# Four stacked graph layers on one core: a score lookup with the table as the stationary operand, edge scores moved into an earlier stage, and another split of the gathered groups

## What is computed

```
xp = (x @ W).reshape(n, 3, 128)
a_src = einsum('nhc,hc->nh', xp, att_src);  a_dst likewise
a_edge = einsum('ehc,hc->eh', (edge_attr @ W_edge), att_edge)     # edge_attr has 16 columns
alpha = a_src[row] + a_dst[col] + a_edge;  alpha = leaky_relu(alpha, 0.2)
m = segment_max(alpha, col);  ex = exp(alpha - m[col]);  attn = ex / segment_sum(ex, col)[col]
agg = segment_sum(attn * xp[row], col)
out = layer_norm(x + agg.reshape(n, 384) @ lin_W + lin_b)
```

## Time and profile before

| | us |
|---|---|
| median of three runs | 3340.34 |
| lowest and highest run | 3336.01, 3341.25 |
| profiled execution, first to last instruction | 3527.6 |
| PE busy in it | 2502.7 (71%) |
| DVE busy | 1567.2 (44%) |
| POOL busy | 1419.9 (40%) |
| ACT busy | 704.3 (20%) |

### The profile page before, as it was taken

How to read it: one execution, slowest core, us unless ns; L and a number is a source line. 1 busy time by engine, 2 the same in 40 slices (tenths; PEclk the granted TensorE clock), 3 DMA queues, 4 the chain that set the end, 5 groups by cost and what they waited for, 6 DMA issues and landing times. The chain is left out here.

```text
span 3527.6 us, 68807 instructions
## 1 busy us (share of the span) xinstructions
PE 2502.7 (71%) x21724; PEld 2132.1 (60%) x21725; DVE 1567.2 (44%) x3759; ACT 704.3 (20%) x1093; POOL 1419.9 (40%) x1498
## 2 busy tenths in 40 slices
PE   1599999898899828999699815555555105888865
PEld 0466666686788617888588714444444105888854
DVE  5476766333111461111333345555545662444467
ACT  0187878353100321000100000000000010000033
POOL 4322222123000031222244466666665786666655
PEclk9899999998999959999899956666666555555577
DMA  4388888722988348888699846555555344555511
GB/s 123 95 251 284 283 275 283 251 73 57 288 284 281 107 124 266 250 246 248 194 287 296 236 139 142 132 137 136 134 134 138 96 128 115 128 128 129 131 41 43
DMA packets 560770, 627.34 MB, mean 178 GB/s; under 512 B 265887, under 2 KB 412524, under 8 KB 560041
## 3 DMA queue, kind: packets, MB, share of 16 engines
q1 hardware_dynamic: 258425, 387.60, 35.8%
q10 hardware_dynamic: 252072, 164.25, 17.0%
q0 software_dynamic: 50208, 74.70, 9.1%
HBM read 484.61 MB, written 142.11 MB: 178 GB/s over the span
## 5 line engine op out<-in xcount | busy, mean ns | idle before, releaser
L893 POOL DMA_INDIRECT rows<-x_rows,src_i x832 | 842.9, 1013 | 477.0 <-issue 224.3
L1567 PE MATMUL ps<-slices,wide 128*128 128x250 f16 x7350 | 829.2, 271 | 57.6 <-DVE wide L2246 34.1
L1567 PEld LDWEIGHTS ps<-slices,wide 128*128 128x128 f16 x7350 | 716.4, 98 | 146.1 <-DVE wide L2246 50.4
L1792 PE MATMUL ps<-slices 128*128 128x75 bf16 x4992 | 343.3, 242 | 340.3 <-issue 324.4
L1792 PEld LDWEIGHTS ps<-slices 128*128 128x128 bf16 x4992 | 294.2, 127 | 389.4 <-issue 388.4
L933 POOL TENSOR_TENSOR ea_one<-ea,ones 128x64 f32<-128x64 f32 x250 | 134.0, 537 | 459.9 <-DMA ea<-in_edge_attr 450.3
L1507 PE MATMUL ps<-weighted,slices 128*128 128x57 f32 x1120 | 254.4, 418 | 82.0 <-issue 72.6
L1507 PEld LDWEIGHTS ps<-weighted,slices 128*128 128x128 f32 x1120 | 247.4, 332 | 83.4 <-issue 73.9
L1453 PE MATMUL ps<-rows,weighted 128*32 128x128 f32 x2000 | 273.3, 281 | 14.8 <-DMA ea<-in_edge_attr 12.9
L1453 PEld LDWEIGHTS ps<-rows,weighted 128*32 128x32 f32 x2000 | 203.1, 112 | 60.3 <-issue 51.9
L2546 DVE TENSOR_TENSOR hT<-ps,hT 128x600 f32<-128x600 f32 x104 | 81.1, 780 | 324.5 <-remote 229.3
(11 more groups left out here) (356 smaller groups left out, 3463.4 us busy)
## 6 DMA issues: line engine op xcount, KB each, us to landing
slices<-adjacency SPq DMA_DIRECT2D x525, 437.5 KB, 4.5
rows<-in_edge_attr SPq DMA_DIRECT2D x250, 256.0 KB
adjacency<-wide ACTq DMA_DIRECT2D x91, 437.5 KB, 3.2
adjacency<-slices ACTq DMA_DIRECT2D x84, 437.5 KB, 3.1
x_of_edges<-rows SPq DMA_DIRECT2D x140, 256.0 KB
slices<-x_of_edges ACTq DMA_DIRECT2D x140, 256.0 KB
slices<-src_low ACTq DMA_DIRECT2D x52, 512.0 KB
rows<-x_rows,src_i POOLq DMA_INDIRECT x832
```

What stands on the lines that cost most here:

```text
L893: pool.indirect_dma_start(out=packed[i][:, c, :], out_offset=None, in_=table, in_offset=bass.IndirectOffsetOnAxis(ap=rows_of, axis=0)).the ...
L1567: mm = pe.matmul(ps_d[b], high_low[:, part, QS * s + q, :], slices[:, s, PN * q:PN * (q + 1)], start=(s == 0 and q == 0 and part == 0), st ...
L1792: mm = pe.matmul(ps_g[:, s, b, c, 0:HEADS * QH], lowT[:, s, b, h, P * c:P * (c + 1)], tab_b[:, n, h, :, :].rearrange("p h i -> p (h i)"), ...
```

## The change

1. **Score loop.** The score table, scaled by a power of two and cut into two f16 parts, is now the stationary operand: 128 table rows by 102 columns (QR = 2 parts x 3 heads x 17), in KT = 3 tables. The one-hots of 512 edges are the moving operand. A step has 12 such matmuls and 4 more (`sum_picks`) that add the picked values up over partitions. DVE's part of a step is three comparisons of [128 x 2048] in f16 (`lows`) and two fused compare-and-multiply instructions of [102 x 1024] (`picked`). ACT copies the sums [12 x 512] out of PSUM and stores them in three DMAs. ACT's queue now also broadcasts the high part of the sources to 102 partitions (`load_hi`).
2. **Edge scores** are made in the second dense product, in 26 pieces of [128 x 3 x 32 x 16] on DVE, two instructions each; SP loads 32 edges for each partition per piece (two DMAs) ahead of the slices, and waits for `es_made` first. They are added after the loop, as are the source scores.
3. **Gather.** The wait of POOL for `scores_begun` is gone. STORED is 108, FRESH is 100; the sum stage takes eight stored groups, then 25 rounds of 8 in which every second is fresh.
4. Around it: the lists of low and high parts are made at the start with seven DVE instructions in place of three; a bound for the scale is worked out before the second product (`score_scale`); a few buffers share memory; POOL sets up a few more constants.

```
-    KT = 2
-    QH = 25
+    KT = 3
+    QH = 17
+    QR = 2 * HEADS * QH
-    FRESH = 68
+    MIXED = NP
+    FRESH = RING * MIXED
-    MIX = 3 * RING
+    MIX = 2 * RING
...
                 def body(q, u, b, first):
+                    if k == 1:
+                        if not first:
+                            sp.wait_ge(es_made, 2 * q - 3)
+                        load_ea(q, b)
                     for s in range(SL):
...
                 if g >= STORED + RING:
-                    pool.wait_ge(group_summed, SUMMED + place(0, 3 * (g - RING - STORED) + 2) + 1)
-                if SCORES_LEAD <= g < SCORES_LEAD + PASSES:
-                    pool.wait_ge(scores_begun, g - SCORES_LEAD + 1)
+                    pool.wait_ge(group_summed, SUMMED + place(0, 2 * (g - RING - STORED) + 1) + 1)
...
+            def store_as(k, s, first=False):
+                u = 2 * k + s
+                act.wait_ge(picks_summed, 2 * u + 2)
+                if not first:
+                    act.wait_ge(as_stored[s], 16 * HEADS * k)
+                act.activation(as_o[:, s, :], ps_o[s], ACT.Copy).then_inc(as_copied, 1)
+                act.wait_ge(as_copied, u + 1)
+                for h in range(HEADS):
+                    act.dma_start(as_d[h:h + 1, bass.ds(SB * u, SB)].rearrange("h (j e) -> (h j) e", e=SQ), as_o[4 * h:4 * (h + 1), s, :]
+                                  ).then_inc(as_stored[s], 16)
+            def next_scores(k, s, first=False):
+                u = 2 * k + s
+                act.wait_ge(lowT_ready, u + 1)
+                load_low(u + 2, s)
+                act.wait_ge(picked_ready, 2 * u + 2)
+                load_hi(u + 2, s)
+                store_as(k, s, first)
...
+            def score_rows(u, s, b, first):
+                pe.wait_ge(lowT_ready, u + 1)
+                if not (first and s == 0):
+                    pe.wait_ge(picked_ready, 2 * u + b - 1)
+                for h in range(KT):
+                    for c in range(2):
+                        mm = pe.matmul(ps_g[:, b, SQ * c:SQ * (c + 1)], tab_b[:, h, :, :, :].rearrange("p n h i -> p (n h i)"),
+                                       lowT[:, s, h, SH * b + SQ * c:SH * b + SQ * (c + 1)], start=(h == 0), stop=(h == KT - 1))
                 mm.then_inc(g_summed, 1)
+            def score_pass(u, s, first):
+                score_rows(u, s, 0, first)
+                if not (first and s == 0):
+                    sum_picks(u - 1, 1 - s, 1, first)
+                score_rows(u, s, 1, first)
+                sum_picks(u, s, 0, first)
...
+            def edge_scores(c, u, i):
+                v.wait_ge(es_in[i], 32 * (u + 1))
+                v.tensor_tensor(es_prod, ea_c.unsqueeze(1).to_broadcast([P, HEADS, ESC, EF]),
+                                we_b[:, :, :].unsqueeze(2).to_broadcast([P, HEADS, ESC, EF]), ALU.mult).then_inc(es_made, 1)
+                v.wait_ge(es_made, 2 * c + 1)
+                v.tensor_reduce(es[:, :, bass.ds(ESC * c, ESC)], es_prod, AX.X, ALU.add).then_inc(es_made, 1)
...
             def score_step(k, s, first=False, last=False):
                 u = 2 * k + s
                 if not (last and s == 1):
                     lows(16 * (k + 1 + s), 1 - s)
-                for b in range(2):
-                    v.tensor_tensor(sel[:, b, :, :], key[:, bass.ds(NC * u + BC * b, BC)].unsqueeze(2).to_broadcast([P, BC, QH]),
...
+                v.wait_ge(hi_in[s], 16 * (k + 1))
                 for b in range(2):
                     v.wait_ge(g_summed, 2 * u + b + 1)
+                    if not (first and s == 0):
+                        v.wait_ge(picks_summed, 2 * u + b - 1)
+                    v.scalar_tensor_tensor(picked[:, b, :], hi_b[:, s, SH * b:SH * (b + 1)], seg_i[0:QR, 0:1], ps_g[:, b, :],
+                                           ALU.is_equal, ALU.mult).then_inc(picked_ready, 1)
```

More of the change, by code:

```diff
@@ L771, in body @@
                     sp.dma_start(xb[:, b:b + 1, :, :], tiles_of(rows_of, q)).then_inc(pair_landed[b], 16)
-                pairs(sp, body)
+                if k == 1:
+                    whole = (E - (P - 1) * EPP) // ESC // 2 * 2
+                    for q in range(2):
+                        body(q, 0, q, True)
+                    with sp.Fori(1, whole // 2) as u:
+                        for b in range(2):
+                            body(2 * u + b, u, b, False)
+                    for q in range(whole, NP):
+                        body(q, q // 2, q % 2, False)
+                    sp.wait_ge(es_made, 2 * NP - 3)
+                    load_ea(NP, NP % 2)
+                else:
+                    pairs(sp, body)
             load_rows_twice(d0, t["x"])
@@ L1689, in _ @@
             pe.wait_ge(prep_dve, NODE_DVE + 3)
+            pe.wait_ge(bound_ready, 1)
+            pe.matmul(ps_m[:, 320:321], ones[:, :], bound[:, 0:1], start=True, stop=True).then_inc(bound_summed, 1)
             missing_groups(missing2_i)
@@ new lines, in sum_picks @@
+            def sum_picks(u, s, b, first):
+                pe.wait_ge(picked_ready, 2 * u + b + 1)
+                if b == 0 and not first:
+                    pe.wait_ge(as_copied, u - 1)
+                for c in range(2):
+                    j = 2 * b + c
+                    mm = pe.matmul(ps_o[s], gather_up[0:QR, j, :], picked[:, b, SQ * c:SQ * (c + 1)], start=(j == 0), stop=(j == 3))
+                mm.then_inc(picks_summed, 1)
+            def score_pass(u, s, first):
[4 more added lines that the diff above has]
+                sum_picks(u, s, 0, first)
@@ L2460, in _ @@
             pairs(v, layer2)
+            edge_scores(NP, NP // 2, NP % 2)
             table_parts(2)
@@ L2633, in _ @@
             lows(16, 0)
-            with v.Fori(0, NIT // 2 - 1) as k:
+            for s in range(2):
+                score_step(0, s, first=True)
+            with v.Fori(1, NIT // 2 - 1) as k:
                 for s in range(2):
-                    score_step(k, s, False)
+                    score_step(k, s)
             for s in range(2):
-                score_step(NIT // 2 - 1, s, True)
+                score_step(NIT // 2 - 1, s, last=True)
+            v.tensor_tensor(AL, FILLP[:, 0:HEADS, :], es, ALU.add).then_inc(dve_step, step.up())
+            v.tensor_copy(XLP, FILLP[:, HEADS:2 * HEADS, :]).then_inc(dve_step, step.up())
             v.wait_ge(as_in, 16)
-            v.tensor_tensor(AL, FILLP[:, 0:HEADS, :], edge_by_edge(AS, HEADS), ALU.add).then_inc(dve_step, step.up())
-            v.tensor_copy(XLP, FILLP[:, HEADS:2 * HEADS, :]).then_inc(dve_step, step.up())
+            v.wait_ge(dve_step, step.n)
+            v.scalar_tensor_tensor(AL, AS, scale3[:, 1:2], AL, ALU.mult, ALU.add).then_inc(dve_step, step.up())
             v.wait_ge(dve_step, step.n)
```

330 lines of the change are left out of this document (163 added, 167 removed).

## The result

The changed kernel takes **3491.74 us** (median of 4 runs, 3488.95 to 3496.73) against 3340.07 us of the kernel before (4 runs): a ratio of 1.0457, interval 1.0444 to 1.0469. It is slower by 151.7 us, and lies 162 us above the top of the predicted range. Its profiled execution took 3489.6 us, about as long as its median. Two spans must therefore not be subtracted; each stage is compared by itself.

A forecast was written before the change was run, and what follows sets the result against it. PE bounded the old sum stage; after the change POOL's gathers would: 29 by 2083, 293 in the loop, 75 until 2601, 544 us for the rest, ending 3151 against 3225. Gain 74 us: 3266 us, range 3125 to 3330.

The forecast's parts named there:

- Edits at nothing: Edge scores in the second dense product and small setup edits cost nothing; 88 us if the cover is gone.
- one of the forecast's own signs of being wrong: List of profile readings that would refute the forecast; among them dense steps over 14.2 us.
- From the profiled execution to the median: Unprofiled runs, 187 us shorter, mostly lack PE's score-loop "issue" time; so the median gains 74 us, not 222.
- Rival 1: PE's "issue" time in the score loop is real, the 187 us lie elsewhere: gain 200 to 222 us, 3130; chance 0.24.
- The sum stage of the kernel before without that time: Old kernel without "issue" time: first fresh group at 2795, then 4 us and 426 us of sums, ending at 3225.
- Rival 4: Sum stage: POOL already the bound, with PE at 2.4 GHz in unprofiled runs; time stays at 3340; chance 0.05.
- the score step: One step of the new score loop, forecast at 7.5 us, so the loop ends at 2473.
- the load chain: ACT's queue in the score loop: the low-parts load waits behind the previous step's store; 4.5 to 10.5 us a step.
- the gather: POOL's gathers carry the sum: 1.25 us each when free, 1.33 us in the score loop.
- rounds of 20 us: Sum stage: each of 25 rounds needs 16 gathers at 1.25 us, 20 us, so POOL is the bound.
- Rival 2: Score loop's load chain is slower, 10.5 us a step, with edge scores that don't hide: 3407 us; chance 0.11.
- rival 3: Score loop: DVE comparisons lock out the gather, losing 110 us of POOL, 82 gathers: 3369 us; chance 0.05.

The follow-up runs named there:

- before_load112: Kernel before plus only the edge-attribute loads in the second dense product, cut into 112 and 15 partitions and read by nothing: 3338.72 us, ratio 1.0002.
- before_again: The kernel before, unchanged, run once more for another profiled execution: 3520.9 us, where the kernel before took 3524.08 us.
- split112_c: split112 run again in a batch where the kernel before took 3517.96 us: 3788.01 us, ratio 1.0776.
- split112: Changed kernel with the 127-partition load of edge attributes cut into two DMAs of 112 and 15 partitions: 3306.82 us, ratio 0.9896 to the kernel before.
- before_order108_d: before_order108 run again, where the kernel before took 3341.21 us: 3308.33 us, ratio 0.9906.
- before_ungated_c: Kernel before with only POOL's wait for `scores_begun` taken out, a repeat in a batch where the kernel before is slow: 3905.14 us.
- before_order108: Kernel before without POOL's wait for `scores_begun` and with the change's group order, where the kernel before took 3524.08 us: 3902.49 us, ratio 1.1077.

## Why the prediction was wrong

- **"Edits at nothing", the edge scores in the second dense product: this step failed.** It counted DVE's time (3.5 us a step, and PE indeed never waited for it), the wait of SP, and the bytes (0.78 to 0.84), and read the last as if a load were spread over all engines whatever its shape. "Seven slices have a whole step to arrive" is true only if the fullest engine carries its part in a step. Its price when the cover is gone, 88 us, was the price of DVE's work; the measured one is 184.9 us, 7.1 us for each step. The term that was missing is the packets on the fullest engine: 127 x 77 to 84 ns against a slack of some 35 packets. It could have been worked out beforehand: `to[0:P - 1]` stands in the diff. One of the forecast's own signs of being wrong caught it: dense steps over 14.2 us, and they are 21.1.
- **From the profiled execution to the median: the step was right, its reason wrong.** I took the 187 us for PE's "issue" time and left it out of the runs that are compared. They do have none of it, and before_load112, which has none either, ends its sums at 3180 instead of 3373. But I held the time to be the profiler's, and cited the Trainium skill (NOTIFIC — the notification-queue block, § 7.1) for it. before_again ran 3520.9 us beside unprofiled runs of 3524 us: the time is real, in some batches. The rule isn't refuted, but no run here shows it at work. So the step came out right for a wrong reason. Rival 1 had the issue time right as real, but placed the 187 us elsewhere, and its gain of 200 us didn't come. In the batches that have the time, without the load, the change is 7.8% slower (split112_c), which neither foresaw.
- **The sum stage of the kernel before without that time**: the first fresh group was forecast for 2795 and came at about 2804. Then I added the 426 us of the earlier trace rows, a stage measured in a disturbed execution; undisturbed it takes 374 us. So the old kernel's sums end at 3180, not 3225, 23 us after those of split112 in the traces, and the gain in the medians is 32 us instead of 74. This is the term that was mis-sized, by 52 us. PE is idle for 26 us of it instead of 72; why the disturbed execution has more isn't shown. Rival 4 came nearer in the gain, but not by its mechanism: the clock in that stage is 0.50 in the undisturbed execution too, and PE, 93% busy, sets its end.
- **Right**: the score step (7.5 us forecast, 7.25 measured; DVE's longest wait is for the low bits, 152 to 157 us in all, as the load chain has it); the gather (1.33 us forecast in the loop, 377 / 292 = 1.29); rounds of 20 us with POOL as their bound; in split112 the last gather at 3150.7 (forecast 3145), the sums' end at 3157 (3151), the span 3313.5 us (3306). So but for the load the forecast of the changed kernel's stages held. The forecast of the median, 3266 us, did not: split112 takes 3306.82, since it was reached by a gain over the kernel before, and that kernel's sum stage was mis-sized.
- **Rival 2, slower**, had the right sign and the clause "with edge scores that don't hide", at 0.11; its mechanism, the load chain of the score loop, and its price of 3407 us were not what happened.
- **Two loose readings, without effect on the sum.** Of the 141.1 us of POOL's waits, 89.5 are named "remote" and only 51.6 the score matmuls. In rival 3 the gather that lost 0.35 us lay beside 1.14 us of comparisons (2380.35 to 2381.49), not 1.22.

DVE's longest wait in the new score loop, from the waits of the changed kernel, 2283 to 2660:

```profile
DVE slices L2616 <- DMA wide<-src_low: 156.7, 49, 5.5
```

## What to carry to other kernels

Ask of each DMA that is added beside a bandwidth-bound stage how many engines it is spread over, not only how many bytes it has: by the rule above a partition count that is prime or has only small divisors puts its packets on few engines (127 and 122 here), and what follows on those engines waits. Cut off the remainder (112 and 15 in place of 127) and check that the landing time of the other transfers stays as it was. And before two times are compared, see that the profile comes from an execution that took as long as the runs: if it doesn't, take another before any stage of it goes into a sum.

The best version found, where the kernel before takes 3340 us, is split112 (0.9896) or, with far less change, before_order108_d (0.9906), the same within their intervals. Where the kernel before takes 3525 us, both are 8 to 11% slower than it, and no version that was run there beats it.

## What the runs showed of the hardware

- One DMA of 254 KB to 127 partitions had one packet in flight at a time for over 10 us, and the issue of the next DMA on the same queue then took 7.76 us (7.9 us in the median of 26), in place of 0.23 us in split112: the queue of the issuing engine stands still as well.
- In some batches PE got one instruction per 1.40 us while POOL gathered beside the score loop, and ran free as soon as POOL stopped; the same program in other batches showed none of it (PE waited for "issue" in its score matmuls for 695.5 us in before_ungated_c; the same kernel has 530.4 us of it as before_order108, 3902.49 us, and none as before_order108_d, 3308.33 us). In the sum stage, where POOL gathers too, no such pitch was seen: 1298 matmuls beside 205 gathers from 3250 to 3650 in before_ungated_c. What sets the batches apart, and what the gather takes from PE, is open.
